# A fused embedding, scan, attention and mixture-of-experts kernel: its second expert layer with all products and transposes on 64-row halves of the array

## The chip, the cores and the metric

The kernel runs on one core of one Trainium2 chip. The metric is the device time of one execution in microseconds (us). Three runs gave 484.43, 485.84 and 486.44 us; the median is 485.84 us. The whole kernel works in float32, apart from small one-hot products in bfloat16.

## The reference, cut to what matters

Eight samples with 64 image patches and 128 text tokens each give 1536 tokens of width 192. They pass through a rotation scan, a first mixture of experts, a linear attention, and a second mixture of experts, the one that is changed:

```python
# D_MODEL 192, D_FF 768, 8 experts, top 2; t = 1536 tokens
xn    = layernorm(x, gamma, beta)
probs = softmax(xn @ router_w)            # (t, 8), two experts kept and renormalised
for e in range(8):
    h = gelu(xn @ w1[e])                  # (t, 192) @ (192, 768)
    y = h @ w2[e]                         # (t, 768) @ (768, 192)
    out += gate[:, e] * y
```

## The kernel before, in words

**Routing.** Each token has two experts. The kernel sorts the 3072 (token, expert) pairs by expert on the chip and fills tiles of 128 rows, each tile of one expert only. There are always 31 tiles (NT), some with padding rows. The expert number of a tile stands in the tensor `et` and is read at run time.

**One tile of the second layer** goes through these engines. All loops are written out, so the program holds every instruction of all 31 tiles.

- GpSimd (POOL) gathers the 128 rows of the tile from DRAM with an indirect DMA (`gather`, L672) into one of four buffers `xs`.
- TensorE (PE) transposes them (`t_x`, L1802 and L1803): columns 0 to 127 and 128 to 255 of the row. The second transpose yields the last 64 features twice, on partitions 0 to 63 and 64 to 127.
- VectorE (DVE) copies the result out of PSUM with the scale and shift of the layer norm (`evac_x`, L1447 to L1451) into `xTs`.
- DVE (L1458) and ScalarE (ACT, L967) each copy half of the tile's first weights from the resident `w1b`, at an address that depends on the expert, to a fixed buffer `w1r` (two of them).
- PE computes the hidden values (`g1`): six products with 128 contracted rows (L1827), then three pairs of products with 64 contracted rows, one on the upper and one on the lower half of the array at the same time (L1831). A float32 product is two matrix instructions, each with its own weight load.
- ACT applies the gelu from two PSUM banks to `hT2` (`nonlin`, L959 and L960).
- PE computes the output (`g2`, L1853): six products with 128 contracted rows and 192 moving columns into bank 6. The moving operand is read straight from the resident `w2b` at an address computed in registers.
- DVE scales the rows with the gate (`evac_y`, L1476) into one of four buffers `ys`, and frees bank 6 with the semaphore `y_ev`.
- POOL adds the rows to the output in DRAM with an indirect DMA that accumulates (`scatter`, L686). A token occurs in two tiles, so `scatter(i)` first waits (L685) until `scatter(i-1)` has landed.

**The order on each engine is written by hand.** PE in step i: `t_x(i+2)`, `g1(i+1)`, `g2(i)`. DVE: `evac_x(i+2)`, `copy_w(i+2)`, `evac_y(i)`. ACT: `copy_w(i+2)`, `nonlin(i+1)`. POOL: `gather(i+6)`, `scatter(i)`, where `gather(j)` waits for `evac_x(j-4)` and `evac_y(j)` waits until `scatter(j-4)` has landed. The expert weights are loaded by SyncE (SP, L552 to L556) long before, during the attention, behind the first half of the loads of the first expert layer's results (`load_acc`, L501); ACT issues the other half.

Of the kernel before, what the change touches and what calls it, by code (L numbers as in the profile page):

```python
# [24 lines left out]
F32 = mybir.dt.float32  # L25
# [7 lines left out]
P = 128  # L33
# [17 lines left out]
W1R = HID1 + HID1 // 2  # L51
# [31 lines left out]
def build(nc, x, out):  # L83
    ctx = ExitStack()
    with ctx:
# [19 lines left out]
        D2 = 2 * P + TOPK  # L105
# [44 lines left out]
        gb2 = sb("gb2", [P, 2, 2])  # L150
# [91 lines left out]
        reg3 = sb("reg3", [P, 2 * HID1 + RING * (D + D2)])  # L242
# [57 lines left out]

        oneA = reg3[:, 0:NA * P // 2].bitcast(BF16).rearrange("p (a r) -> p a r", a=NA)
# [13 lines left out]
        bank = [ctx.enter_context(nc.psum_tensor(f"bank{i}", [P, 512], F32)) for i in range(8)]  # L315
# [39 lines left out]
        w1r_act = sem("w1r_act"); w1r_dve = sem("w1r_dve")  # L355
# [24 lines left out]
        LG_BANK = 6  # L380

# [123 lines left out]
        def _(sp):  # L505
# [53 lines left out]
            sp.dma_start(tok_rows(xd[1][:, D:2 * P]), xn[:, :, P:D]).then_inc(xd_written, 16)  # L559
            sp.wait_ge(gate_ready, 1)  # L560
            sp.dma_start(tok_rows(xd[1][:, 2 * P:D2]), gate2[:, :, :]).then_inc(xd_written, 16)
# [164 lines left out]
        def _(act):  # L726
# [223 lines left out]
            def experts(l, func, hid):  # L950
# [12 lines left out]
                def copy_w(i, p):  # L963
# [5 lines left out]
                                         ACT.Copy).then_inc(w1r_act, 1)  # L969

# [3 lines left out]
                if l:  # L974
                    act.wait_ge(ld_ffn1, 16 * 4 * NE)
                    copy_w(0, 0)
                    copy_w(1, 1)
                nonlin(0, 0)

                for i in range(NT):  # L980
# [89 lines left out]
        def _(dve):  # L1070
# [363 lines left out]
            def experts(l, hid, hc):  # L1434
                nhc = hid // hc

                def evac_x(i, p):

                    dve.wait_ge(tx_mm, l * NT + i + 1)
                    src = bank[p][:, 0:2 * P].rearrange("p (k t) -> p k t", k=NK)  # L1440
                    if l == 0:
                        V.tensor_copy(xTs[0:KC, p, :, :], src[0:KC]).then_inc(tx_ev, 1)
                    else:
                        dst = xTs[:, p, :, :]

                        row = xs[:, i % RING, 2 * P:D2]
# [20 lines left out]
                def evac_y(i):  # L1467
# [220 lines left out]
        def _(pe):  # L1688
# [95 lines left out]
            def experts(l, hid, hc, w1, w2, biased):  # L1784
                nhc = hid // hc
                w1v = w1.rearrange("p e k f -> p (e k f)") if l == 0 else None
                w2v = w2.rearrange("p e c n -> p (e c n)")
# [4 lines left out]
                def t_x(i):  # L1792
# [7 lines left out]
                    else:  # L1800

                        nc.tensor.transpose(bank[s % 2][:, 0:P], xs[:, s, 0:P], ident)  # L1802
                        ins = nc.tensor.transpose(bank[s % 2][:, P:2 * P], xs[:, s, P:2 * P], ident)  # L1803
                    ins.then_inc(tx_mm, 1)

                def g1(i, p, e):
# [14 lines left out]
                    half = nhc // 2  # L1821

                    def h_of(c):
                        return bank[2 + 2 * p + c // half][:, (c % half) * P:(c % half + 1) * P]

                    for c in range(nhc):
# [479 lines left out]
```

## Time and profile before

| | |
|---|---|
| median of three runs | 485.84 us |
| the profiled execution, first to last instruction (its span) | 471.0 us |
| what lies around the span: median less span | 14.8 us |
| mean granted TensorE clock | 0.944 |
| instructions in the profile | 8360 |
| PE busy in the span | 417.4 us |
| second expert layer in the span | from about 314.5 us to the end |

The profiled execution has no separate device time beside its span; the 14.8 us are the distance between the span and the median of the timed runs. A time such as 327.00 is counted from the start of the span. Busy time of matrix instructions overlaps (their ends are modelled), so the distance between starts tells more than their durations.

### The profile page before, as it was taken

To read this page: it belongs to the slowest core of one execution; us is meant where nothing else is said; L and a number is where in the kernel's file an instruction comes from. 1 tells how busy PE (TensorE), PEld (TensorE's weight loads), DVE (VectorE), ACT (ScalarE), POOL (GpSimd) and SP (SyncE) were. 2 spreads that over 40 slices of the span, in tenths; PEclk is the share of its full clock that TensorE was granted. 3 is DMA by queue.
4 is the path that set the end of the run, shared out by engine and by line. 5 is a ranking of instruction groups with operands and counts; after the bars stand their busy time and mean duration, and the time that the engine had idled before them with its cause. 6 is when DMAs were issued, how large, how long until landed. Compare 5 with 4: busy or idle time off the path is not lost.

```text
span 471.0 us, 8360 instructions
## 1 busy us (share of the span) xinstructions
PE 417.4 (89%) x2603; PEld 330.6 (70%) x2609; DVE 275.7 (59%) x1304; ACT 170.4 (36%) x350; POOL 221.9 (47%) x265
## 2 busy tenths in 40 slices
PE   4897768899967999999789889879999999999991
PEld 4643634646634888888647779438999999999981
DVE  3889999899783544544395358964434343343420
ACT  1189976361461111111136014463232323323220
POOL 3300389999025777775300002245555654564532
PEclk9898769999888999999799999979999999999997
DMA  8439000000052222222399900592323322332222
GB/s 253 65 82 248 4 0 3 1 33 2 1 156 59 66 80 77 76 79 64 92 324 316 289 12 2 118 132 68 58 42 59 49 51 41 60 50 43 39 26 26
DMA packets 38046, 38.20 MB, mean 81 GB/s; under 512 B 7547, under 2 KB 34159, under 8 KB 38003
## 3 DMA queue, kind: packets, MB, share of 16 engines
q1 hardware_dynamic: 26486, 22.13, 18.8%
q0 software_dynamic: 9312, 14.03, 14.9%
q10 hardware_dynamic: 2204, 1.49, 1.1%
q8 instruction: 23, 0.38, 0.3%
q14 instruction: 21, 0.16, 0.1%
HBM read 27.28 MB, written 10.37 MB: 80 GB/s over the span
## 4 chain that ended last, share of the span: by engine, by line
PE 64%; DVE 15%; ACT 10%; DMA 7%; issue 2%; POOL 1%; POOLq 0%; ACTq 0%; SPq 0%; DVEq 0%
PE bank L1853 21%; PE bank L1827 9%; PE bank L1812 7%; PE bank L1831 6%; DVE bank L1226 2%; DVE reg L1219 2%; PE bank L1839 2%; DMA xn_rows<-gate 2%; ACT reg L794 2%; DMA a<-expert_rows 2%; PE bank L1707 2%; ACT xn L762 2%; PE bank L2055 2%; PE bank L1798 2%; DVE st L1095 1%
## 5 line engine op out<-in xcount | busy, mean ns | idle before, releaser
L1853 PE MATMUL bank<-reg 128*128 (+1 forms) x558 | 104.8, 333 | 1.5 <-DVE reg L1465 0.7
L1853 PEld LDWEIGHTS bank<-reg 128*128 128x128 f32 (+1 forms) x558 | 89.4, 190 | 12.0 <-issue 8.0
L686 POOL DMA_INDIRECT out<-reg,idxs x31 | 49.4, 1594 | 62.7 <-DMA out<-reg,idxs 41.1
L672 POOL DMA_INDIRECT reg<-xn_rows,idxs x62 | 60.8, 981 | 28.4 <-issue 15.5
L1476 DVE TENSOR_SCALAR reg<-bank,gs 128x192 f32<-128x192 f32 x31 | 12.9, 418 | 86.1 <-PE bank L1853 86.1
L959 ACT ACTIVATE reg<-bank 128x384 f32<-128x384 f32 x31 | 15.2, 490 | 97.8 <-PE bank L1831 97.8
L1827 PE MATMUL bank<-xTs,xT 128*128 128x128 f32 x372 | 46.7, 275 | 0.0
L1827 PEld LDWEIGHTS bank<-xTs,xT 128*128 128x128 f32 x372 | 44.0, 192 | 0.0
L680 POOL DMA_INDIRECT expert_rows<-reg,idx x31 | 30.6, 987 | 16.9 <-DVE reg L1474 9.9
L955 ACT ACTIVATE reg<-bank 128x288 f32<-128x288 f32 x31 | 12.7, 410 | 70.6 <-PE bank L1812 70.6
L1226 DVE TENSOR_REDUCE bank<-reg 128x6 f32<-128x24 f32 x272 | 37.7, 184 | 0.2 <-issue 0.2
L1812 PE MATMUL bank<-reg,xTs 96*128 (+1 forms) x124 | 36.3, 415 | 0.0
L1695 PE MATMUL bank<-con 128*128 128x512 bf16 x136 | 35.0, 416 | 0.7 <-issue 0.5
L1474 DVE COPY reg<-bank 128x192 f32<-128x192 f32 x31 | 11.1, 357 | 35.4 <-PE bank L1853 35.4
L1831 PE MATMUL bank<-xTs,xT 64*128 64x128 f32 x372 | 29.1, 289 | 0.0
L1895 PE MATMUL bank<-xT,wst 96*128 96x512 f32 (+1 forms) x48 | 25.6, 689 | 3.7 <-ACT xT L812 2.8
L1695 PEld LDWEIGHTS bank<-con 128*128 128x128 bf16 x142 | 15.2, 111 | 18.2 <-issue 6.0
L713 POOL TENSOR_SCALAR onep<-rs 128x3 f32<-128x3 f32 x4 | 0.9, 228 | 56.4 <-DVE nm L1107 56.4
L641 POOL TENSOR_TENSOR reg<-reg 128x128 f32<-128x128 f32 x63 | 26.2, 455 | 1.8 <-PE bank L1988 1.8
L1831 PEld LDWEIGHTS bank<-xTs,xT 64*128 64x128 f32 x372 | 23.2, 187 | 3.7
L1812 PEld LDWEIGHTS bank<-reg,xTs 96*128 96x128 f32 (+1 forms) x124 | 21.7, 195 | 3.5
L1219 DVE TENSOR_TENSOR reg<-reg,bank 128x24 f32<-128x24 f32 x176 | 23.7, 175 | 0.1
(351 smaller groups left out, 775.4 us busy)
## 6 DMA issues: line engine op xcount, KB each, us to landing
reg<-in_w2b SPq DMA_DIRECT2D x8, 576.0 KB, 7.2
reg<-in_w1b SPq DMA_DIRECT2D x8, 384.0 KB, 7.4
reg<-in_w1a SPq DMA_DIRECT2D x8, 216.0 KB
reg<-in_w2a SPq DMA_DIRECT2D x8, 216.0 KB
xn_rows<-xn SPq DMA_DIRECT2D x4, 384.0 KB, 2.7
reg<-in_w1b SPq DMA_DIRECT2D x16, 96.0 KB, 6.5
xn_rows<-xn SPq DMA_DIRECT2D x1, 1152.0 KB, 7.9
out<-h SPq DMA_DIRECT2D x1, 1152.0 KB, 10.8
```

The lines of the kernel that those rows point to most:

```text
L641: ins = nc.gpsimd.tensor_tensor(term[b % 2][k][:, 0:n, :, r, :], second[:, :, :, r, k:k + 1].to_broadcast([P, n, NCH, 4]), first[:, :, :, ...
L672: pool.indirect_dma_start(xs[:, i % RING, 0:(D, D2)[l]], None, xd[l], bass.IndirectOffsetOnAxis(ap=idxs[:, i:i + 1], axis=0)).then_inc(xs_ ...
L680: pool.indirect_dma_start(ybuf, bass.IndirectOffsetOnAxis(ap=idx2[:, i:i + 1], axis=0), ys[:, i % RING, :], None).then_inc(scat[i % RING], 16)
L686: pool.indirect_dma_start(out, bass.IndirectOffsetOnAxis(ap=idxs[:, i:i + 1], axis=0), ys[:, i % RING, :], None, compute_op=ALU.add).then_ ...
L1219: V.tensor_tensor(prodv[:, ch], entries[:, ch], slot(t)[:, ch].unsqueeze(2).to_broadcast([P, 2, 3, 4]), ALU.mult).then_inc(scan_self[half], 1)
L1226: V.tensor_reduce(slot(t)[:, ch, 0:3], prodv[:, ch], AX, ALU.add).then_inc(scan_self[half], 1)
L1695: MM(bank[bk][:, :], con[:, 0:P // 2].bitcast(BF16), con[:, 0:2 * P].bitcast(BF16), start=True, stop=True)
L1812: ins = MM(bank[2][:, 0:hid], xTs[0:r, p, k, :], w1v[0:r, bass.ds(e * (NK * hid) + k * hid, hid)], start=(k == 0), stop=(k == NK - 1))
L1827: MM(h_of(c), w1r[:, p, c * hc:(c + 1) * hc], xTs[:, p, 0, :], start=(c % half == 0), stop=False)
L1831: ins = MM(h_of(c + half * a), w1r[rs, p, HID1 + c * hc:HID1 + (c + 1) * hc], xTs[rs, p, 1, :], start=False, stop=(c == half - 1))
L1853: ins = MM(bank[6][:, 0:D], (hTs if l == 0 else hT2[:, p])[0:r, c * P:(c + 1) * P], w2v[0:r, bass.ds(e * (nhc * D) + c * D, D)], start=(c ...
L1895: ins = MM(bank[UB[u]][:, :], wst[0:r, k, cc, :], xT[0:r, k, 512 * g:512 * g + 512], start=(k == 0), stop=(k == NK - 1))
```

## The change

The second expert layer uses only products and transposes of 64 contracted rows, in pairs on the upper and lower half of the array.

- `t_x` of layer 1: six transposes of 64 tokens by 128 columns in place of two of 128 by 128, into two neighbouring banks. The row in DRAM now ends in a copy of features 0 to 63 in place of 128 to 191, so the lower half holds the features in another order than the upper one. There is one pair of banks for all tiles but the second, so `t_x(i)` waits for `evac_x(i-1)`.
- `evac_x` of layer 1: three scalings of 128 partitions by 2 x 64 in place of two of 128 by 128, into a new buffer `xT64`.
- `g1`: nine pairs of 64-row products in place of six whole products and three pairs. The resident `w1b` has another order, loaded by three DMAs as before, of which the first is now 64 partitions by three pieces.
- `g2`: six pairs of 64-row products into banks 6 and 7 in place of six whole products into bank 6. The moving operand comes from a fixed buffer `w2r`, to which ACT copies the tile's second weights (128 partitions by 1152 elements). The expert number is no longer read on PE.
- `evac_y`: a second instruction adds bank 7 to the scaled bank 6, after a wait for the first.

```diff
+        DX = D + 64
+        D2 = DX + TOPK
@@ SP
             for e in range(NE):
-                sp.dma_start(w1b[:, e, 0:HID1], x["w1b"][e][0:P, :]).then_inc(ld_ffn1, 16)
-                for a in range(2):
-                    fs = slice(a * HID1 // 2, (a + 1) * HID1 // 2)
-                    sp.dma_start(w1b[64 * a:64 * a + 64, e, HID1:W1R], x["w1b"][e][P:D, fs]).then_inc(ld_ffn1, 16)
+                part = w1b[:, e, :].rearrange("p (k f) -> p k f", k=NK3)
+                src = x["w1b"][e].rearrange("(k p) f -> p k f", p=64)
+                sp.dma_start(part[0:64], src[:, :, 0:HALF1]).then_inc(ld_ffn1, 16)
+                sp.dma_start(part[64:P, 0:2], src[:, 1:3, HALF1:HID1]).then_inc(ld_ffn1, 16)
+                sp.dma_start(part[64:P, 2:3], src[:, 0:1, HALF1:HID1]).then_inc(ld_ffn1, 16)
@@ ACT
+                def copy_w2(i, p, e):
+                    if i >= 2:
+                        act.wait_ge(g2_mm, l * NT + i - 1)
+                    nc.scalar.activation(w2r[:, p, :],
+                                         w2b.rearrange("p e c n -> p (e c n)")[:, bass.ds(e * W2R, W2R)],
+                                         ACT.Copy).then_inc(w2r_act, 1)
...
                 for i in range(NT):
                     if l and i + 2 < NT:
-                        copy_w(i + 2, i % 2)
+                        e = copy_w1(i + 2, i % 2)
                     if i + 1 < NT:
                         nonlin(i + 1, (i + 1) % 2)
+                    if l and i + 2 < NT:
+                        copy_w2(i + 2, i % 2, e)
@@ DVE
-                        V.tensor_scalar(dst[:, 0, :], src[:, 0, :], gb2[:, 0, 0:1], gb2[:, 1, 0:1], ALU.mult, ALU.add)
-                        V.tensor_scalar(dst[:, 1, :], src[:, 1, :], gb2[:, 0, 1:2], gb2[:, 1, 1:2],
-                                        ALU.mult, ALU.add).then_inc(tx_ev, 1)
+                        for k in range(NK3):
+                            ins = V.tensor_scalar(dst[:, k], src[:, :, 64 * k:64 * k + 64], gb2[:, 0, k:k + 1],
+                                                  gb2[:, 1, k:k + 1], ALU.mult, ALU.add)
+                        ins.then_inc(tx_ev, 1)
...
-                        V.tensor_scalar(ys[:, s, :], bank[6][:, 0:D], gs[:, i:i + 1], None,
-                                        ALU.mult).then_inc(y_ev, 1)
+                        link(V.tensor_scalar(ys[:, s, :], bank[6][:, 0:D], gs[:, i:i + 1], None, ALU.mult))
+                        V.scalar_tensor_tensor(out=ys[:, s, :], in0=bank[7][:, 0:D], scalar=gs[:, i:i + 1],
+                                               in1=ys[:, s, :], op0=ALU.mult, op1=ALU.add).then_inc(y_ev, 1)
@@ PE
-                        nc.tensor.transpose(bank[s % 2][:, 0:P], xs[:, s, 0:P], ident)
-                        ins = nc.tensor.transpose(bank[s % 2][:, P:2 * P], xs[:, s, P:2 * P], ident)
+                        if i >= 2:
+                            pe.wait_ge(tx_ev, NT + (i if i > 2 else 1))
+                        dst = two_banks[X_BANKS[i == 1]]
+                        for k in range(NK3):
+                            for a in range(2):
+                                rs = slice(64 * a, 64 * a + 64)
+                                ins = nc.tensor.transpose(
+                                    dst[:, a, 64 * k:64 * k + 64],
+                                    xs[rs, s, 64 * k:64 * k + P],
+                                    con[rs, C_ID + 64 * a:C_ID + 64 * a + 64])
...
-                    for c in range(nhc):
-                        MM(h_of(c), w1r[:, p, c * hc:(c + 1) * hc], xTs[:, p, 0, :], start=(c % half == 0), stop=False)
-                    for c in range(half):
-                        for a in range(2):
-                            rs = slice(64 * a, 64 * a + 64)
-                            ins = MM(h_of(c + half * a), w1r[rs, p, HID1 + c * hc:HID1 + (c + 1) * hc],
-                                     xTs[rs, p, 1, :], start=False, stop=(c == half - 1))
+                    for c in range(nhc // 2):
+                        for k in range(NK3):
+                            for a in range(2):
+                                rs = slice(64 * a, 64 * a + 64)
+                                col = k * HALF1 + c * hc
+                                ins = MM(bank[2 + 2 * p + a][:, c * P:(c + 1) * P], w1r[rs, p, col:col + hc],
+                                         xT64[rs, p, k, :], start=(c == 0 and k == 0),
+                                         stop=(c == nhc // 2 - 1 and k == NK3 - 1))
...
+                        for a in range(2):
+                            rs = slice(64 * a, 64 * a + 64)
+                            ins = MM(bank[6 + a][:, 0:D], hT2[rs, p, c * P:(c + 1) * P],
+                                     w2r[rs, p, c * D:(c + 1) * D],
+                                     start=(c == 0), stop=(c == nhc - 1))
```

## Rows read from the trace of the kernel before

**Rows 1.** The page: span, PE's share, and the chain that ended last, by engine.
```profile
span 471.0 us, 8360 instructions
...
PE 417.4 (89%) x2603; PEld 330.6 (70%) x2609; DVE 275.7 (59%) x1304; ACT 170.4 (36%) x350; POOL 221.9 (47%) x265
...
PE 64%; DVE 15%; ACT 10%; DMA 7%; issue 2%; POOL 1%; POOLq 0%; ACTq 0%; SPq 0%; DVEq 0%
```

**Rows 2.** The chain in order of time, one tile: start, us, what.
```profile
381.15 0.11 PE bank L1802
381.26 0.11 PE bank L1803
381.37 1.34 PE bank L1827 x12
...
382.71 0.87 PE bank L1831 x12
383.58 2.15 PE bank L1853 x12
```

**Rows 3.** The same chain, its end.
```profile
461.66 0.43 DVE reg L1476
...
462.32 3.45 DMA out<-reg,idxs
```

**Rows 4.** The waits from 318 us on: us in total, times, longest.
```profile
POOL out L686 <- DMA out<-reg,idxs: 41.1, 21, 3.4
POOL out L686 <- DVE reg L1476: 19.1, 9, 4.3
```

**Rows 5.** The timeline of POOL: start, us, then in brackets the idle time before.
```profile
327.00 1.63 POOL L686 DMA_INDIRECT out<-reg,idxs  x1 [2.30 <-DVE reg L1476]
331.57 1.59 POOL L686 DMA_INDIRECT out<-reg,idxs  x1 [1.64 <-DVE reg L1476]
...
345.29 1.58 POOL L686 DMA_INDIRECT out<-reg,idxs  x1 [1.70 <-DVE reg L1476]
...
350.85 1.59 POOL L686 DMA_INDIRECT out<-reg,idxs  x1 [2.68 <-DMA out<-reg,idxs]
...
373.62 1.63 POOL L686 DMA_INDIRECT out<-reg,idxs  x1 [1.51 <-DMA out<-reg,idxs]
375.55 0.99 POOL L672 DMA_INDIRECT reg<-xn_rows,idxs  x1 [0.30 <-issue]
378.00 1.59 POOL L686 DMA_INDIRECT out<-reg,idxs  x1 [1.45 <-DMA out<-reg,idxs]
...
462.32 1.55 POOL L686 DMA_INDIRECT out<-reg,idxs  x1 [2.69 <-DVE reg L1476]
466.53 1.55 POOL L686 DMA_INDIRECT out<-reg,idxs  x1 [2.66 <-DMA out<-reg,idxs]
```

**Rows 6.** The chain in order of time, where the attention switches row size.
```profile
244.57 0.87 PE bank L2062 x8
245.44 1.52 PE bank L2055 x8
```

**Rows 7.** Groups of instructions by shape, from 320 us on: busy us, mean ns.
```profile
L967 ACT ACTIVATE xT<-reg 128x576 f32 x29 | 19.8, 684 | 0.1
L959 ACT ACTIVATE reg<-bank 128x384 f32<-128x384 f32 x31 | 15.2, 490 | 97.8 <-PE bank L1831 97.8
...
L1458 DVE COPY xT<-reg 128x576 f32 x29 | 14.8, 511 | 0.5 <-issue 0.5
L1476 DVE TENSOR_SCALAR reg<-bank,gs 128x192 f32<-128x192 f32 x31 | 12.9, 418 | 86.1 <-PE bank L1853 86.1
L1450 DVE TENSOR_SCALAR xTs<-bank,gb 128x128 f32<-128x128 f32 x30 | 12.1, 405 | 0.0
```

**Rows 8.** The DMA view from 345.29 to 471 us: packets, MB, share of the engines.
```profile
q8 instruction: 9, 0.15, 0.4%
```

**Rows 9.** The DMA view from 427 to 428.2 us, same columns.
```profile
q0 software_dynamic: 142, 0.10, 81.3%
q8 instruction: 1, 0.02, 5.0%
```

**Rows 10.** The DMA view from 233 to 272 us: issues, KB each, us to landing.
```profile
reg<-in_w1b SPq DMA_DIRECT2D x8, 384.0 KB, 7.4
```

More of the change, by code:

```diff
@@ L50 @@
 HC0, HC1 = 96, 128
-W1R = HID1 + HID1 // 2
+NK3 = D // 64
+HALF1 = HID1 // 2
+W1R = NK3 * HALF1
 NH, HD = 12, 16
@@ L297, in build @@
         assert o <= NR2
+        o = 0
+        xT64 = carve(reg2, 2 * NK3 * P).rearrange("p (b k t) -> p b k t", b=2, k=NK3)
+        W2R = HID1 // HC1 * D
+        w2r = carve(reg2, 2 * W2R).rearrange("p (b f) -> p b f", b=2)
+        assert o <= NR2
         oneA = reg3[:, 0:NA * P // 2].bitcast(BF16).rearrange("p (a r) -> p a r", a=NA)
@@ L313, in build @@
         ys = carve(reg3, RING * D).rearrange("p (s n) -> p s n", s=RING)
-        bank = [ctx.enter_context(nc.psum_tensor(f"bank{i}", [P, 512], F32)) for i in range(8)]
+        psum = ctx.enter_context(nc.psum_tensor("bank", [P, 8 * 512], F32))
+        bank = [psum[:, 512 * i:512 * (i + 1)] for i in range(8)]
+        two_banks = [psum[:, 1024 * i:1024 * (i + 1)].rearrange("p (s c) -> p s c", s=2) for i in range(4)]
         ld_con = sem("ld_con"); ld_lab = sem("ld_lab"); ld_ids = sem("ld_ids"); ld_seg = sem("ld_seg")
@@ L380, in build @@
         LG_BANK = 6
+        X_BANKS = (0, 2)
         TB = (0, 1, 4, 5)
@@ L961, in nonlin, with copy_w1 @@
                                              func).then_inc(act_done, 1)
-                def copy_w(i, p):
+                def copy_w1(i, p):
                     e = act.value_load(et[0:1, i:i + 1], min_val=0, max_val=NE - 1)
@@ L975, in experts @@
                     act.wait_ge(ld_ffn1, 16 * 4 * NE)
-                    copy_w(0, 0)
-                    copy_w(1, 1)
+                    e0 = copy_w1(0, 0)
+                    e1 = copy_w1(1, 1)
+                    copy_w2(0, 0, e0)
                 nonlin(0, 0)
+                if l:
+                    copy_w2(1, 1, e1)
                 for i in range(NT):
                     if l and i + 2 < NT:
-                        copy_w(i + 2, i % 2)
+                        e = copy_w1(i + 2, i % 2)
                     if i + 1 < NT:
                         nonlin(i + 1, (i + 1) % 2)
+                    if l and i + 2 < NT:
+                        copy_w2(i + 2, i % 2, e)
             for ch in range(NCH):
@@ L1851, in g2 @@
                     for c in range(nhc):
-                        r = hc + 1 if (c == nhc - 1 and biased) else hc
-                        ins = MM(bank[6][:, 0:D], (hTs if l == 0 else hT2[:, p])[0:r, c * P:(c + 1) * P],
-                                 w2v[0:r, bass.ds(e * (nhc * D) + c * D, D)],
-                                 start=(c == 0), stop=(c == nhc - 1))
+                        if l == 0:
+                            r = hc + 1 if (c == nhc - 1 and biased) else hc
+                            ins = MM(bank[6][:, 0:D], hTs[0:r, c * P:(c + 1) * P],
+                                     w2v[0:r, bass.ds(e * (nhc * D) + c * D, D)],
+                                     start=(c == 0), stop=(c == nhc - 1))
+                            continue
+                        for a in range(2):
+                            rs = slice(64 * a, 64 * a + 64)
+                            ins = MM(bank[6 + a][:, 0:D], hT2[rs, p, c * P:(c + 1) * P],
+                                     w2r[rs, p, c * D:(c + 1) * D],
+                                     start=(c == 0), stop=(c == nhc - 1))
                     ins.then_inc(g2_mm, 1)
@@ L1865, in experts @@
                 for i in range(NT):
-                    nxt = expert_of(i + 1) if i + 1 < NT else None
+                    nxt = expert_of(i + 1) if l == 0 and i + 1 < NT else None
                     if i + 2 < NT:
```

32 lines of the change are left out of this document (16 added, 16 removed).

## The prediction, on record before the result

> **What bounds the kernel now.** I read the page first. It says that PE is busy 89% of the span and holds 64% of the chain that ended last [rows 1]; taken alone, that promises that a faster PE is a faster kernel. The change touches the time only after 314.5 us, so the second view is the chain in order of time. There every tile takes the same five pieces, 0.11 + 0.11 + 1.34 + 0.87 + 2.15 = 4.58 us, without a gap [rows 2], and again it is all PE. But the end of the chain leaves PE: the last output is scaled at 461.66 us, and 3.45 us of a DMA `out<-reg,idxs` and one more scatter follow [rows 3].
>
> So the third view is the waits: POOL's scatter (L686) waited 41.1 us in 21 waits for the DMA of the scatter before it, and only 19.1 us in 9 waits for the scaled rows [rows 4]. The fourth, the timeline of POOL, gives the pace. The first four intervals are 4.57 us, PE's pace (327.00, 331.57, three more up to 345.29). Later ones that waited for the DMA are 378.00 - 373.62 = 4.38 us, and at the end, with no gather between, 466.53 - 462.32 = 4.21 us [rows 5]. The scatter's own landing thus allows no tile in less than about 4.37 us with a gather and 4.26 without (means of the undisturbed ones), and PE stands only 0.2 us above it. Five of the 30 intervals are far longer: 5.56 (345.29 to 350.85 in rows 5), and 5.33, 6.32, 5.44 and 7.14 us, together 7.9 us over 4.37. After each the scatters are behind PE and run at DMA pace. From 327.00 to 466.53 the 30 intervals sum to 139.53 us: 24 x 4.37 + 6 x 4.26 = 130.4, plus 7.9 of the five long ones, plus about 1.0 where PE was the slower, and 0.2 of rounding. That last 1.0 us is all that a faster PE can take out of this chain. The reader is to see that PE can be 100% busy and yet be no longer what sets the end.
>
> **PE's part of the change.** Half products run in pairs. Three pairs of 128 columns, two instructions each, are 6 slots in 0.87 us, 0.145 a slot; the whole products take 1.34/12 = 0.112 [rows 2]. Per slot the same work is done, so either a pair is dearer, or changing the row size costs. The attention has both sizes with 192 columns: 4 slots of pairs in 0.87, 8 slots whole in 1.52 [rows 6]. If a slot costs s and a change w, 4s + w = 0.87 and 8s + w = 1.52, so s = 0.163 and w = 0.22. In the tile, 6 x 0.112 + w = 0.87 gives w = 0.20, and 12 x 0.163 + w = 2.15 gives w = 0.19. Four equations, one answer: a pair costs as much as a whole product, and each change of size about 0.2 us, twice per tile. The Trainium skill (TensorEngine Tiling (Array Packing), Key Properties) says that changing the tiling mode drains TensorE; the trace agrees, at these 0.2 us.
>
> After: `g1` 18 slots x 0.112 = 2.01; `g2` 12 x 0.163 = 1.95; both changes gone, -0.40. The transposes grow from two slots (0.22) to three pairs; no row has a pair of 64 columns. Lower bound 3 x 0.055 = 0.17 (half of a slot of 0.11), upper 3 x 0.112 = 0.34; the weight load has 128 columns as before, so I take 0.30. PE's tile is 4.26 us (4.13 to 4.30), 0.3 below now, at or under the scatters' 4.37. Over 31 tiles PE alone would gain about 10 us.
>
> **DVE and ACT.** DVE per tile: one more scaling of `bank`, +0.41, and a second instruction in `evac_y`, +0.42 and 0.1 for the wait between [rows 7]; about 2.1 before, 3.0 of 4.37 after. It lies in DVE's idle time (86.1 us in front of L1476 now). ACT: two gelus 0.98, `w1` copy 0.68, and the new copy of 1152 elements. Two `w1` copies would be 1.37; from 384 to 576 elements the rows rise by 0.19, so it is at least 0.68 + 3 x 0.19 = 1.26; I take 1.3. Sum 2.95. Its order matters: `copy_w2(i+2)` waits for `g2(i)`, behind it stand `copy_w1(i+3)` and `nonlin(i+2)`. From the end of `g2(i)`, 1.3 + 0.7 = 2.0 us pass, while PE needs 0.3 + 2.0 for `t_x(i+3)` and `g1(i+2)` before that gelu can start. The cover is some 0.3 us per tile; if it is gone, each missing 0.1 us is late at the next tile's `g2`, one step further on, and is then hidden by PE's own `g2`.
>
> The new wait of `t_x(i)` for `evac_x(i-1)` has `g1` and `g2` queued behind it. `evac_y` and `evac_x` end about 2.5 us after the transposes and the wait comes 4.3 us after them: 0. `gather(j)` waits for `evac_x(j-4)`, later by 0.9 us; POOL stands 1.45 us before each scatter anyway [rows 5]. At the start `evac_x(0)` is 0.3 us longer and visible, two `g1` and a `g2` save 0.6 to 0.8 with their four changes less three longer `t_x`, and the first `evac_y` is 0.5 longer: the first scatter moves by +0.15 us.
>
> **SP's queue** has as many DMAs; those of `w1b` have 1536-byte rows in place of 3072. They take until 272 us in both [rows 10] and are needed at 314.57; the cover is 40 us. They share the engines with the loads of the first layer's results around 241 us; smaller packets there are worth at most 0.2 us either way. 0.
>
> **What is late next: the scatter chain.** y-limited intervals gone: -1.0. First scatter: +0.15. Then the five long intervals. Four of them hold a transfer on q8, the queue that brings instructions, in the middle of the scatter's 142 packets [rows 9], and some rows of the scatter land late. There are 9 such transfers of 16 KB between 345 and 471 us [rows 8], one per 2.9 tiles. PE has 76 matrix instructions a tile now and 132 after (12 + 72 + 48), while some 13 for register work go: I reckon about 89 against 137 in all, so about 15.5 transfers over the scatters in place of 10. The Trainium skill (Runtime: NRT & Kernel Launch, Instruction fetch mechanics) says that instructions come in 16 KiB blocks of 256; this trace's 13.3 us between blocks and 89 instructions per tile agree. The same section calls the crossing mostly hidden; that it can delay another queue's scatter is this trace's finding, as a coincidence in time only.
>
> The price of one is bounded from both sides. The four with a transfer cost 1.2, 1.0, 1.95 and 2.8 over pace, 6.9 over 10 transfers, 0.7 each; at that price 15.5 cost 10.8, +3.9. But seven of the ten fell in the second part of the scatter's cycle, where they hit; with a step of 1.87 tiles they spread over all phases, and a transfer of 1 us can hit in about half the cycle at 0.8 on average: 0.4 each, 6.2, -0.7. Between -0.7 and +3.9 I take +1.5.
>
> **Sum.** -1.0 + 0.15 + 1.5 = +0.65 us: span 471.65, and with the 14.8 us around it 486.5 us. Own range 484 to 489.5.
>
> **The rivals.**
> 1. *PE still sets the end.* For: 64% of the chain [rows 1]. Against: 21 of 31 scatters waited for the DMA. Then 31 x 0.3 = -9.5: 476.5 us; nearly as low if the long intervals vanished as well as the 1.0 (-6.9 - 1.0): 478. Together 0.06.
> 2. *Instruction transfers hit at the old rate.* +3.9 - 0.85: 489 us, slower. Decides from about 0.6 us per transfer on. For: seven of ten hit or nearly did. Chance 0.23.
> 3. *The pair itself is dear, not the change of size.* Then 0.145 x 21 + 0.2175 x 12 = 5.66 us per tile, 31 x 1.08 = +33: 519 us. Against: the four equations. A milder form, PE's instruction supply failing with 132 in place of 76 a tile, would show from 4.4 us per tile on; the first 24 of L1831 run within 0.75 us. At 4.7 us per tile the end is at 490 us. Together 0.08.
> 4. *The transfers mostly miss, or fewer scatters are disturbed:* 482.5 us, 0.13.
>
> **How the numbers follow.** About 0.5%, 2.4 us, is what a measurement of this kernel can tell from no change. My forecast has 0.50, rivals 1 to 4 have 0.06, 0.23, 0.08 and 0.13. Faster: rival 1 and most of 4, 0.16. Slower: rivals 2 and 3, most of them, and the upper edge of my forecast, 0.32. The same: 0.52. The range from 482.8 to 490.0 leaves out rival 1, the low part of 4 and the dear pairs.
>
> **What the profile after will show.** Right: no change of size in the tile, `g1` about 2.0 and `g2` 1.95 between starts; `t_x` 0.3; PE with gaps before its transposes, since gathers arrive with the scatters; scatters at 4.37 us nearly from the start and hardly a wait for DVE; 15 or 16 transfers on q8 after 327 us; the last scatter 0 to 3 us later than 466.5. Wrong: if intervals under 4.2 us appear, the landing is no floor and the time falls towards 477; if the PE tile is over 4.4, its supply or ACT's copy is the new bound; if ACT starts its gelu long after `g1` ends, `copy_w2` is in the way; if q8 has more transfers but the long intervals do not follow them, my term of +1.5 falls and the time is 485.0.

## The result, and the profile after

The change took 486.77 us (median of 12 runs, 484.20 to 488.61) against 485.25 us before (12 runs, 483.42 to 486.44): ratio 1.0038, 95% interval 1.0021 to 1.0056. On another chip, where the kernel before takes 471.49 us (35 runs), the change took 472.48 us (12 runs): ratio 1.0016, 0.9985 to 1.0047. One of these 12 runs took 681.75 us at a mean granted clock of 0.56, a disturbed state that is left out of the ratio; the others took 470.15 to 476.03 us at 0.93 to 0.95. Both ratios are within the 0.5% that I called no change, though the first interval reaches just over it and leaves out 1.

The page of the changed kernel, whose profiled execution took 487.99 us; it answers to [rows 1]:

```profile
span 486.1 us, 9977 instructions
...
PE 411.7 (85%) x3477; PEld 327.9 (67%) x3477; DVE 296.4 (61%) x1366; ACT 206.4 (42%) x381; POOL 222.9 (46%) x265
...
PE 51%; DVE 15%; ACT 11%; DMA 9%; issue 7%; another core or an unknown queue 5%; POOLq 0%; POOL 0%; SPq 0%; DVEq 0%; ACTq 0%
```

The chain in order of time, one tile; it answers to [rows 2]:

```profile
358.45 0.18 PE bank L1845 x6
358.63 2.06 PE bank L1871 x36
360.70 1.95 PE bank L1903 x24
```

The same chain, its end; it answers to [rows 3]:

```profile
458.46 3.51 DMA out<-reg,idxs
...
462.72 5.33 DMA out<-reg,idxs
...
468.80 3.50 DMA out<-reg,idxs
...
473.05 3.48 DMA out<-reg,idxs
...
477.28 3.49 DMA out<-reg,idxs
```

The waits from 324 us on; they answer to [rows 4]:

```profile
POOL out L704 <- DMA out<-reg,idxs: 45.6, 23, 4.5
POOL out L704 <- DVE reg L1511: 9.9, 6, 2.4
POOL out L704 <- issue: 5.4, 2, 2.8
```

The reader is to see three things. The tile on PE is three pieces, 0.18 + 2.06 + 1.95 = 4.19 us, where it was five of 4.58. The end of the chain is now one landing of a scatter after another, with nothing of PE between them, while PE's last product is over at 466.5 us (from there to the end the view by stretches counts no matmul) and the last scatter is issued at 481.53. And 23 of the 31 scatters wait for the DMA of the one before, 6 for the scaled rows, and 2 for nothing that the profile shows.

The span is 15 us longer than that of the kernel before and says nothing about the change: all 15 us lie ahead of layer 2 (the first gather of layer 2 at 314.49 us before, 329.51 after), where the two kernels differ only in the order of the loads of `w1b` and in the last columns of the stored rows. 12.2 of the 15 us lie between the first and the last store of the first expert layer (75.2 us before, 87.5 after). Experiments 1 and 5 show that this is not the change: on their chips the same stretch takes 75.2 us in either kernel. The profile shown before must have come from a chip like theirs. From the first gather of layer 2 to the end the two spans have 156.50 and 156.54 us.

### The profile page after: what moved, and what is told of

It reads as the page before. It is cut to its first block, busy times and chain, and to the rows that moved or that the text cites. A ratio compares the mean times of both kernels' runs of the same rounds, so it can differ in the third digit from the quotient of the medians.

```text
span 486.1 us, 9977 instructions
## 1 busy us (share of the span) xinstructions
PE 411.7 (85%) x3477; PEld 327.9 (67%) x3477; DVE 296.4 (61%) x1366; ACT 206.4 (42%) x381; POOL 222.9 (46%) x265
## 3 DMA queue, kind: packets, MB, share of 16 engines
q1 hardware_dynamic: 27510, 22.13, 20.2%
## 4 chain that ended last, share of the span: by engine, by line
PE 51%; DVE 15%; ACT 11%; DMA 9%; issue 7%; another core or an unknown queue 5%; POOLq 0%; POOL 0%; SPq 0%; DVEq 0%; ACTq 0%
PE bank L1871 11%; PE bank L1903 10%; DMA out<-reg,idxs 6%; PE bank L1896 5%; PE bank L1857 4%; DVE bank L1258 2%; DVE reg L1251 2%; ACT reg L812 2%; PE bank L1880 2%; PE bank L1945 2%; PE bank L2105 2%; DMA con<-in_consts 1%; ACT reg L962 1%; PE bank L1730 1%
## 5 line engine op out<-in xcount | busy, mean ns | idle before, releaser
L1871 PE MATMUL bank<-reg,xT 64*128 64x128 f32 x1116 | 70.7, 275 | 0.6 <-DVE reg L1484 0.6
L1903 PE MATMUL bank<-reg 64*128 64x192 f32 x744 | 67.0, 323 | 1.1 <-DVE reg L1511 1.1
L1871 PEld LDWEIGHTS bank<-reg,xT 64*128 64x128 f32 x1116 | 66.4, 188 | 0.9 <-DVE reg L1484 0.7
L1903 PEld LDWEIGHTS bank<-reg 64*128 64x128 f32 x744 | 61.1, 187 | 1.3 <-issue 1.3
L994 ACT ACTIVATE reg<-reg 128x1152 f32 x31 | 36.1, 1165 | 30.4 <-PE bank L1903 28.9
L973 ACT ACTIVATE reg<-bank 128x288 f32<-128x288 f32 x31 | 12.7, 411 | 83.7 <-PE bank L1857 59.8
L1896 PE MATMUL bank<-reg 96*128 x186 | 37.5, 339 | 7.0 <-DVE reg L1499 6.5
L1896 PEld LDWEIGHTS bank<-reg 96*128 96x128 f32 x186 | 30.5, 194 | 15.2 <-issue 14.8
L1730 PE MATMUL bank<-con 128*128 128x512 bf16 x142 | 37.8, 427 | 0.0
L1484 DVE TENSOR_SCALAR reg<-bank,gb 128x128 f32<-128x128 f32 x93 | 32.4, 404 | 0.0
L1730 PEld LDWEIGHTS bank<-con 128*128 128x128 bf16 x142 | 15.5, 113 | 19.0 <-issue 7.4
```

The lines of the kernel that those rows point to most:

```text
L994: nc.scalar.activation(w2r[:, p, :], w2b.rearrange("p e c n -> p (e c n)")[:, bass.ds(e * W2R, W2R)], ACT.Copy).then_inc(w2r_act, 1)
L1484: ins = V.tensor_scalar(dst[:, k], src[:, :, 64 * k:64 * k + 64], gb2[:, 0, k:k + 1], gb2[:, 1, k:k + 1], ALU.mult, ALU.add)
L1730: MM(bank[bk][:, :], con[:, 0:P // 2].bitcast(BF16), con[:, 0:2 * P].bitcast(BF16), start=True, stop=True)
L1871: ins = MM(bank[2 + 2 * p + a][:, c * P:(c + 1) * P], w1r[rs, p, col:col + hc], xT64[rs, p, k, :], start=(c == 0 and k == 0), stop=(c == n ...
L1896: ins = MM(bank[6][:, 0:D], hTs[0:r, c * P:(c + 1) * P], w2v[0:r, bass.ds(e * (nhc * D) + c * D, D)], start=(c == 0), stop=(c == nhc - 1))
L1903: ins = MM(bank[6 + a][:, 0:D], hT2[rs, p, c * P:(c + 1) * P], w2r[rs, p, c * D:(c + 1) * D], start=(c == 0), stop=(c == nhc - 1))
```

## The experiments

All ran on chips where the kernel before takes 471.5 to 473.3 us, so they are compared with it and with each other, not with the 486 us above. Tiles and scatters are counted from 0. "Layer 2" is the stretch from its first gather to the end of the span.

**1. The kernel before, once more.** No edit.

> The kernel before once more, unchanged, for a second trace. The trace shown of it has a span of 471.0 us against a median of 485.25, while the changed kernel's has 486.1 us against its own execution's 487.99. In that trace the tiles of the first expert layer (unchanged code) ran at 2.52 us each, in the changed kernel's at about 3.05. Theory A: the first trace of the kernel before is simply an execution whose first expert layer ran without its usual waits, and a second trace has a span near 483 us with tiles near 3.0 us there, and a second expert layer of 156 to 158 us from the first gather to the end. Theory B: the first layer is slower because of the change (+15 us there, with a gain of as much hidden elsewhere); then the second trace has again about 471 us and 2.52 us a tile.

Measured: 470.54 us, span 468.7 us. So 1.8 us lie around the span, not 14.8. Theory A falls: the span is again about 470 us and a tile of the first expert layer takes 2.51 us, as theory B says. But the cause that theory B gives falls with experiment 5, where the changed kernel too has 2.51 us a tile and a span of 469.1 us. The 15 us between the two profiles go with the chip; what on the chip makes them is not known. Layer 2 takes 155.65 us here (first gather at 313.10 us), the first scatter comes 12.62 us behind the gather, and the 30 intervals between scatters sum to 138.53 us.

**2 and 3. The chain taken away, before and after.** In both, layer 2 stores its rows as layer 1 does, each row to a place of its own in `expert_rows`, without waiting for the scatter before. The adding into `out` is left out. The edit, the same in both:

```
-                    if l == 0:
+                    if True:
                         pool.indirect_dma_start(ybuf, ...idx2[:, i:i + 1]...)
                         return
```

Of the kernel before:

> The kernel before with the second layer's scatter made a plain one into the scratch rows of the first layer, so that no scatter waits for the one before it (left out: the adding of the expert rows to the output). Theory S (the chain of accumulating scatters sets the end): PE's end plus one short scatter is left, some 4 us less than before, 481 us. Theory P (PE set the end all along): the same 4 us or less, since only the last landing gets shorter; so this one alone does not tell them apart, the next one does.

Of the changed kernel:

> The changed kernel with the same plain scatter, no chain (left out: the adding of the expert rows). Theory S: the whole saving of PE comes out. In the changed kernel's trace PE ends at 466.4 us and the last scatter starts at 481.5; without the chain the end is near 471.5, 14.5 us less: 472 us, and 9 to 10 us under the unchained kernel before. Theory P: no more is freed than in the kernel before, 482 us, the same as the unchained kernel before within 1 us.

Measured: 467.64 us (ratio to before 0.9933, 0.9906 to 0.9960) and 458.42 us (0.9710, 0.9686 to 0.9735). The difference between the two is 9.2 us. Layer 2 takes 151.3 and 141.1 us. The end of the chain of the second:

```profile
450.44 1.97 PE bank L1903 x24
452.41 0.03 issue
452.44 0.43 DVE reg L1510
452.86 0.02 issue
452.89 0.43 DVE reg L1511
453.32 0.27 issue
453.58 0.97 POOL expert_rows L698
```

The last store but one goes out 1.2 us behind its product. The stores follow each other at TensorE's pace, 4.57 us in the kernel before and 4.20 in the changed one. Without the chain TensorE sets the end in both kernels, and the 9 to 10 us that the change saves appear. With the chain it is hidden: the kernel before has 4 us between itself and its unchained form, the changed kernel 14 us.

**4. More instructions on TensorE, first try.** 48 `pe.nop()` per tile in the kernel before.

> The kernel before with 48 empty instructions (no operation) in PE's stream after each tile's last product, so that its stream has as many instructions per tile as the changed kernel's (137 in place of 89) and q8 brings about 16 blocks over the scatters in place of 10, with the same work on PE. Theory S with my term for the instruction transfers: the scatters are disturbed more often, +1.5 us (0 to +4), 486.8 us. Rival: transfers on q8 only coincide with long intervals; no change, 485.3 us within 0.5, and as many long intervals as before. If PE's tile gets longer than 4.58 us the run says nothing on this.

Measured: 472.21 us, ratio 1.0005 (0.9982 to 1.0029). The added instructions are not in the program that ran: TensorE's count is that of the kernel before, and q8 has the same 10 transfers among the scatters. The run is one more of the kernel before and decides nothing about the transfers.

**5. The change, on this chip.** No edit.

> The changed kernel as it is, timed beside the kernel before on this chip. Theory S (the chain of accumulating scatters sets the end, so what TensorE saves is hidden): ratio to before 1.000 to 1.005, so on a chip where before takes 471.7 us the change takes 472 to 474. Rival P (the change's gain shows when the earlier part of the program runs undisturbed): ratio 0.98 to 0.99, TensorE being 10 us shorter. In both, the chain of layer 2 from the first gather to the end takes 156 to 157 us.

Measured: 472.48 us, ratio 1.0016. Layer 2 takes 154.59 us, 1.1 less than in experiment 1. The first scatter comes 12.61 us behind the gather, the intervals sum to 137.42 us. The first rows of POOL's timeline:

```profile
327.12 1.63 POOL L704 DMA_INDIRECT out<-reg,idxs  x1 [2.10 <-DVE reg L1511]
331.56 1.59 POOL L704 DMA_INDIRECT out<-reg,idxs  x1 [1.50 <-DVE reg L1511]
335.94 1.57 POOL L704 DMA_INDIRECT out<-reg,idxs  x1 [1.49 <-DVE reg L1511]
340.24 1.58 POOL L704 DMA_INDIRECT out<-reg,idxs  x1 [1.43 <-DMA out<-reg,idxs]
```

The intervals are 4.44, 4.38 and 4.30 us where they were 4.57 [rows 5], and from the fourth scatter on POOL waits for the DMA. The scaled rows of scatter 3 are ready 0.80 us ahead of it, those of scatter 30 12.65 us. The theory of the chain holds; that the gain shows when the earlier part runs undisturbed is excluded, since 0.98 would be 462 us.

**6. The second products whole again.** Six products of 128 rows into one bank, one eviction; the first products and the transposes stay as the change has them.

```
-                        for a in range(2):
-                            rs = slice(64 * a, 64 * a + 64)
-                            ins = MM(bank[6 + a][:, 0:D], hT2[rs, p, ...], w2r[rs, p, ...], ...)
+                        ins = MM(bank[6][:, 0:D], hT2[:, p, ...], w2r[:, p, ...], ...)
```

> The second products go back to six whole 128-row products into one bank with one eviction; the pairs of the first products and of the transposes stay. Theory S with the delay of the first scatter (0.87 us in the change, of which the second eviction of y and the pairs' later end are a part): the first scatter comes some 0.3 to 0.5 us sooner and the time is 0.3 to 0.8 us under the change's. The pairs of the second products cost TensorE as much as six whole ones at the row rate (1.95 us a tile in either form), so TensorE's tile stays 4.2 to 4.3 us or gets longer by at most 0.3. Rival (the pairs of the second products save what the change gains): TensorE's tile 4.5 us or more, and the time is that of the change or over it.

Measured: 472.18 us, ratio 1.0013 (0.9981 to 1.0045). One tile of the chain:

```profile
386.04 0.33 PE bank L1844 x6
386.37 2.06 PE bank L1870 x36
388.44 2.15 PE bank L1900 x12
```

The tile is 4.54 us, 0.35 more than with pairs, and by number this is what I had written for the rival. Its cause is not the one given there. The twelve slots of whole rows cost 2.15 us and the 24 instructions in pairs 1.95; the six transposes in front, which are the same instructions as in the change, rise from 0.18 to 0.33 us. Two changes of row size are back in the tile, at 0.20 and 0.15 us, one in each direction. My expectation had left them out, although the prediction had them. The first scatter did not come sooner (12.88 us). And with a tile longer by 0.35 us the time is the same: the 30 intervals sum to 137.43 us. The make-up of the sum is another: here 15 scatters wait for the scaled rows, and only two intervals are over 4.9 us where in experiment 5 six are. The landings that come late sum to 1.7 us here and 4.4 there. That the two cancel is not shown to be more than chance.

**7. Two sums.** The change, with the scatters of odd tiles adding into an array `out_odd` of their own and added to `out` at the end. Each scatter then waits for the one two before it.

```
-                    if i:
-                        pool.wait_ge(scat[(i - 1) % RING], 16 * (turns(l, i - 1) + 1))
-                    pool.indirect_dma_start(out, ...)
+                    if i >= 2:
+                        pool.wait_ge(scat[(i - 2) % RING], 16 * (turns(l, i - 2) + 1))
+                    pool.indirect_dma_start((out, out2)[i % 2], ...)
...
+            wait_scatters(pool, 1)
+            for q in range(2):
+                rs = slice(q * NTOK // 2, (q + 1) * NTOK // 2)
+                pool.dma_start(out[rs, :]..., out2[rs, :]..., accum_op=ALU.add).then_inc(comb, 16)
```

> The change, with the scatters of odd tiles adding into a second array of their own, so that each waits for the one two before it; at the end two accumulating transfers add the second array to the output. Theory S: the scatters follow the tiles at TensorE's 4.2 us, the last goes out 1.5 to 3 us behind the last product, and the time up to there is 9 to 11 us shorter than the change's; the sum at the end moves 1.6 MB read twice and written once and costs 5 to 9 us, so the whole is 1 to 5 us under the change. Rival (the Pool engine's own 1.6 us of issue for each scatter and about as much for each gather, or contention of two scatters at once, sets the pace): intervals between scatters stay near 4.4 us and the whole is 4 to 9 us over the change.

The edit also fills `out_odd` with zeros at the start (not shown). Measured: 470.91 us, ratio to before 0.9997 (0.9964 to 1.0030), 1.6 us under the change on the same chip, which is less than the spread of the runs of either. The end of its chain:

```profile
448.40 2.23 PE bank L1913 x24
...
451.80 3.43 DMA out<-reg,idxs
...
455.91 1.83 POOL out L747 x2
```

The last scatter goes out 1.2 us behind the last product, 12.7 us sooner than in experiment 5, and the scatters follow each other at 4.20 us, so the pace of the chain is the landing and not POOL's own issue. But from the landing of the last scatter at 455.2 us to the end of the span the sum takes 12.3 us, where I had expected 5 to 9. What the second array wins, the sum takes back. It does not beat the kernel before.

**8. Instructions on another engine.** The kernel before, with 48 `sp.sem_inc(spare, 1)` behind each tile on the Sync engine.

> The kernel before, with 48 semaphore increments that nobody waits for on the Sync engine behind every tile of layer 2, some 1500 instructions, about as many as the change adds to TensorE. Theory T (a transfer of instructions that meets a scatter makes its interval longer by 0.4 to 0.7 us): 16 instead of 10 such transfers lie among the scatters, and the time is 1 to 3 us longer, ratio 1.002 to 1.006. Rival N (the long intervals have another cause, and these transfers cost nothing that adds up): ratio 0.999 to 1.001, with the extra of the long intervals near 7 us as in the kernel before.

Measured: 472.35 us, ratio 1.0021 (0.9991 to 1.0051), and layer 2 in 155.79 us as in experiment 1. The Sync engine's instructions come on another queue. The page of the kernel before (experiment 1) has, and below it the page of this one:

```profile
q8 instruction: 23, 0.38, 0.4%
q14 instruction: 20, 0.16, 0.1%
```

```profile
q8 instruction: 23, 0.38, 0.3%
q14 instruction: 31, 0.25, 0.2%
```

The ratio alone lies between the two theories. Eleven more transfers of 8 KB on q14, all among the scatters, cost layer 2 nothing that shows (0.14 us); late landings sum to 2.9 us here and 4.1 us in experiment 1. TensorE's 16 KB transfers on q8 were not increased, so the question about them stayed open, but the traces up to here suggested another reading, which the next runs tested.

**9. POOL's instructions shifted.** The change, with 100 `pool.sem_inc(spare, 1)` once ahead of layer 2.

> The change with 100 semaphore increments on the Pool engine that nobody waits for, once, ahead of its part of layer 2. In all traces so far, of either kernel, the interval behind scatter 14 (counted from 0) and that behind scatter 21 are 1.0 to 1.2 us longer than their neighbours though the scatter's transfer lands after the usual 3.5 to 3.6 us and y is ready. Theory F (the Pool engine's own instructions run out there and are brought in late): the two move to other tiles, since the Pool engine's instruction stream is shifted by 100. Rival G (they hang on the count of transfers issued, or on the data): they stay at 14 and 21. In either case the time is that of the change within 1 us, 470 to 474 us where before takes 471.5.

Measured: 471.85 us. The long intervals with a normal landing stayed behind scatters 14 and 21 (5.46 and 5.52 us, landings 3.5 and 3.4). They are not late instructions of POOL; theory F falls.

**10. More instructions on TensorE, second try.** The change, with 36 `pe.sem_inc(spare, 1)` behind each tile.

> The change with 36 more instructions a tile of layer 2 on TensorE (semaphore increments that nobody waits for), 1100 in all, so four to five more 16 KB transfers of instructions on the queue that carries them. Theory T (each such transfer among the scatters costs the chain 0.3 to 0.45 us): 19 to 20 transfers, the chain 1.3 to 2 us longer, ratio to before 1.004 to 1.006. Rival W (only a transfer that starts 1.4 to 3.4 us behind a scatter's issue, while that scatter's own packets move, makes it land about 1.1 us later; others cost nothing): the extra follows the number of those, 3 to 8 of them, and not the total; each of the others leaves a landing of 3.5 to 3.6 us. In both TensorE's tile grows by 36 increments, and if it passes 4.5 us TensorE sets the pace and the time says nothing.

Measured: 624.2 us, ratio 1.322. The increments themselves set the pace. The chain of one tile:

```profile
396.38 3.88 issue
400.26 0.40 PE bank L1845 x6
400.66 3.69 PE bank L1871 x36
404.35 1.95 PE bank L1903 x24
```

Thirty-six of them take 3.9 us, in which TensorE makes no product. The granted clock is still 1.00 from 396.4 to 400.2 us, while they run, and falls behind them: 0.57 from 400 to 404 us, 1.00 from 404 to 406. The first products take 3.69 us in place of 2.06. As the expectation says for a tile over 4.5 us, the time tells nothing of the transfers.

**11. TensorE's instructions shifted.** The change, with 128 such increments once ahead of layer 2.

> The change with 128 more instructions on TensorE (semaphore increments that nobody waits for), once, ahead of layer 2, so that the transfers of its instructions fall half a transfer earlier, between other tiles, with their number (15 to 16 among the scatters) the same. Rival W above: the tiles with late landings (in the change's two traces behind scatters 5, 12, 17 and 22 or 26) move to others, each again with a transfer that starts 1.4 to 3.4 us behind the scatter's issue, and 14 and 21 stay long. If the late landings hang on the tile's data or on memory: they stay at 5, 12 and 17. The time is within 2 us of the change's.

Measured: 486.81 us; the increments delay the start of layer 2 by 15 us (TensorE idle for 14.97 us in front of its first transposes), which the expectation missed by leaving out their price. From the first scatter on it is a clean comparison: 30 intervals in 136.77 us, 15 transfers on q8. The late landings are now behind scatters 6, 13, 18 and 23, where they were behind 5, 12, 17, 22 and 24 in experiment 5. The transfers start 2.24, 2.01, 1.79 and 2.25 us behind the scatter's issue. Rival W holds, and the tile's data as the cause of the late landings is excluded. Scatters 14 and 21 stay followed by long intervals.

**12. POOL's transfers shifted.** The change, with eight more gathers on POOL ahead of layer 2's own.

> The change with eight extra gathers of the same kind ahead of layer 2's own (their data is overwritten by the real ones), which the Pool engine waits for; this delays layer 2 by some 8 us. The late issues behind scatters 14 and 21 stayed there when only instructions were added to the Pool engine. Theory G1 (they hang on the number of transfers that the Pool engine has issued): eight transfers are four tiles' worth, so they come behind scatters 10 and 17. Theory G2 (they hang on the tiles' data, on the time, or on something else in the program): they stay at 14 and 21. The time is 478 to 483 us where before takes 472 in either case.

Measured: 488.82 us. The delay is larger than the 8 us expected: the eight gathers go in two groups of 7 us each, and the first scatter comes 16.6 us later than in experiment 5. The late issue behind scatter 21 is now behind 17 (5.21 us, landing 3.5), four tiles earlier, as theory G1 says. The one behind 14 should be behind 10, and that interval is 4.37 us. The time since the start is no explanation, since in experiment 11 all scatters are 16 us later and the place stays. So one of the two seems to hang on the number of transfers that POOL has issued, though the theory named two places and only one came; of the other no run shows the cause.

## Why the prediction was right

**What bounds the kernel.** Right, and shown by experiments 2 and 3: TensorE's gain of 9 to 10 us is real and lies behind the chain of accumulating scatters.

**PE's tile.** 4.26 us forecast, 4.19 found. `g1` 2.01 forecast and 2.06 found, `g2` 1.95 and 1.95, the two changes of row size gone. The three pairs of transposes cost 0.18 us, next to the lower bound of 0.17 and not the 0.30 that I took. That a pair costs as much as a whole product and a change of size 0.2 us was inferred from four equations [rows 2, 6]; experiment 6 shows it, with the change of size back at 0.20 and 0.15 us. The gaps that I forecast before TensorE's transposes, since gathers would arrive with the scatters, did not come: in the trace of experiment 5 the tiles follow each other at 4.20 us with a single pause, of 1.1 us, and TensorE ends 13.8 us ahead of the last scatter in experiment 5, 3.9 us in experiment 1. So the four buffers on either side cover such a lead.

**DVE and ACT.** Right. ACT's copy takes 1.165 us (forecast 1.3). Its order did no harm: POOL's waits name no ACT, and PE has no gap. DVE's second eviction took nothing from the chain once the scatters were behind.

**SP's queue.** No run separates it. Executions of the same code ahead of layer 2 differ by up to 5 us there (first gather at 313.1 to 316.1 us in the four experiments on the kernel before, at 314.2 to 319.1 in eight on the change), so an effect of one or two us there could not be seen.

**First scatter.** +0.15 us forecast. Compared on like chips it is 12.62 and 12.61 us behind the first gather: 0. In the first profile after it was 13.38, which no other trace of the changed kernel repeats (12.54 with POOL's instructions shifted).

**The intervals that waited for y.** -1.0 us forecast, -0.8 found. From a landing to the next issue POOL takes 0.79 us; what the intervals have beyond landing and this sums to 1.14 us in experiment 1 and 0.33 us in experiment 5 (those behind scatters 14 and 21 left out). The 30 intervals as a whole sum to 138.53 and 137.42 us, -1.1: the other -0.3 is in the landings, late ones +0.3 and ordinary ones -0.6.

**The transfers of instructions.** This is the term that was wrong. The count was right: 15.5 forecast, 16 in the first profile after:

```profile
q8 instruction: 16, 0.26, 0.7%
```

15 in experiment 5, and 10 before. The price was wrong: "Between -0.7 and +3.9 I take +1.5". Two things were thrown together in the five long intervals. Two rows of experiment 5 part them. In the first pair the scatter itself lands late, in the second everything has landed and POOL is still late:

```profile
404.68 1.59 POOL L704 DMA_INDIRECT out<-reg,idxs  x1 [1.44 <-DMA out<-reg,idxs]
...
410.11 1.59 POOL L704 DMA_INDIRECT out<-reg,idxs  x1 [2.55 <-DMA out<-reg,idxs]
...
423.32 1.59 POOL L704 DMA_INDIRECT out<-reg,idxs  x1 [1.55 <-DMA out<-reg,idxs]
...
428.91 1.78 POOL L704 DMA_INDIRECT out<-reg,idxs  x1 [2.70 <-issue]
```

For the scatter at 404.68 us, and then for that at 423.32 us, the view of their line gives

```profile
DMA to landing us min/median/max: 4.6/4.6/4.6
...
DMA to landing us min/median/max: 3.5/3.5/3.5
```

The second kind comes behind scatters 14 and 21 in every trace in which the chain sets the pace and POOL has its own order, before and after alike, at 1.1 and 1.3 us. The one behind 21 is there even without the chain (5.79 and 5.40 us between two stores in experiments 2 and 3). It has nothing to do with the change. Only the first kind belongs to the transfers, and not to their number. I sorted the 114 transfers on q8 that start among the scatters in nine traces with the chain (all but the first of the changed kernel, whose scatters have no landing in that view, and experiments 2, 3, 7 and 10) by how long behind the issue of the last scatter they start, and called a landing late from 0.3 us over 3.55 on:

| start behind the issue, us | transfers | late landings | mean lateness, us |
|---|---|---|---|
| 0 to 1.3 | 35 | 0 | 0.0 |
| 1.3 to 1.9 | 9 | 4 | 0.3 |
| 1.9 to 2.95 | 25 | 24 | 1.0 |
| 2.95 to 3.7 | 34 | 6 | 0.2 |
| 3.7 and over | 11 | 1 | 0.05 |

So a transfer delays a scatter by 1 us if it starts in one particular microsecond of about 4.4, when the scatter's packets begin, which is 0.24 hits for a transfer at a random phase. I had taken half the cycle. Before, 4 of 10 landed in or near it (4.1 us of late landings in experiment 1, 5.6 in the first profile); after, 4 or 5 of 15 (4.5 us in experiment 5, 3.5 in 11). From trace to trace the sum varies by more than this: 2.9 to 6.4 us in the four traces of the kernel before, experiments 4 and 8 among them, and 2.7 to 4.4 in experiments 5, 9, 11 and 12. Over all 114 a transfer cost 0.3 us, under both of my bounds of 0.4 and 0.7. The upper one held some of the second kind (1.3 of the 6.9 us, in the interval of 7.14 us), the lower one gave the hits half of the cycle. The term is 0 or slightly negative in place of +1.5. That was the last of my signs of being wrong: more transfers, but long intervals that do not follow them. Three landings of 3.9 us have no transfer beside them. The Trainium skill (Runtime: NRT & Kernel Launch, Instruction fetch mechanics) gives blocks of 16 KiB, and the traces agree (23 transfers, 0.38 MB); that the phase of a transfer matters and not their number stands on these traces alone.

**The sum.** In layer 2 the forecast was +0.65 us; on like chips it is -1.1 (155.65 to 154.59). This is one trace of each; layer 2 takes 155.6 to 156.7 us in four traces of the kernel before, and 156.5, 154.6 and 153.6 in three of the change (the first profile, experiments 5 and 9). The medians differ by +1.0 us on this chip, where the interval of the ratio is -0.7 to +2.2, and by +1.5 us on the first (+1.0 to +2.7). Half of the +1.0 us is not in the spans at all: their medians are 469.7 and 470.2 us, and around the span the runs of experiment 5 have 1.9 to 3.4 us where those of the kernel before have at most 1.9. The rest of the 2 to 3 us between layer 2 and the whole would lie ahead of layer 2, by subtraction of medians and single traces. Whether this is an effect of the change (its weights come in shorter rows, 27,510 packets in place of 26,486) or only the spread of that part is not settled. That the forecast of 486.5 us came within 0.3 us of the median is thus partly luck: a term too high by at least 1.5 us stood in for something that I had put at 0. By the prediction's own sign above, the time without that term was 485.0 us.

**The 14.8 us around the span.** Wrong as a quantity: they compared a profile of one chip with runs of another. It is 1.8 to 1.9 us on like chips, and in some runs of the change up to 3.4. The 14.8 itself did no harm, since it was added to both kernels.

**The rivals.** That PE still sets the end (476.5 us) is excluded by experiments 3 and 5. That the transfers hit at the old rate (489 us) falls with the table. The dear pair (519 us) is excluded by the tile. That the transfers mostly miss (482.5 us) is nearest to what layer 2 did, at a third of its size.

A version in which a scatter waits only where the expert changes, since the tiles of one expert hold different tokens, might take most of the chain away; experiment 3, without any chain, gives 458 us as the bound. It wasn't tried.

## What to carry to other kernels

Look at what follows the last product before making the products faster: an engine with the largest share of the chain, 64% here, was 0.2 us per tile from the next limit, and some 9 of the 10 us saved went into waiting for a landing. An accumulating scatter that waits for the one before is a clock of its own: 3.5 us of landing and 0.8 us to the next issue here, whatever TensorE did. And before pricing a coincidence in a trace, sort all its occurrences by phase and by kind; five long intervals had two causes, and the price per transfer that I took from them was that of neither.

## What the runs showed of the hardware

- Twenty-four matrix instructions of 64 rows, in pairs, take 1.95 us where twelve of 128 rows take 2.15 with a change of row size ahead of them, and the first instructions after a change of row size are late by 0.15 to 0.20 us (experiment 6).
- A 16 KB transfer of instructions in the way of a scatter makes it land 1.0 us late in 24 of 25 cases if it starts 1.9 to 2.95 us behind the issue, and in none of 35 if it starts in the first 1.3 us. Eleven more 8 KB transfers for another engine cost layer 2 nothing that shows (155.79 us against 155.65).
- A semaphore increment on TensorE that nobody waits for costs 0.11 to 0.12 us (36 in 3.9 us, 128 in 15 us), and behind 36 of them, 3.9 us without a product, the granted clock was 0.57 on average over 4 us, mostly the lower of its two levels (1.2 GHz), before it was 1.00 again (experiment 10). 100 on POOL and 48 a tile on the Sync engine did not lengthen layer 2.
- POOL issues two scatters 1.1 and 1.3 us late at fixed places. With eight gathers put ahead one of the places moved by four tiles, and at the other nothing is late any more, neither there nor four tiles earlier (experiment 12).
- The same program took 471.5 us on one chip and 485.3 us on another (the kernel before), 472.5 and 486.8 (the changed one). In the two profiles of the changed kernel, 486.1 and 469.1 us, 15.0 of the 17 us lie ahead of layer 2, 12.2 of them in the first expert layer.
